# Head of a state-space and expert-routing kernel: unread matrix products in TensorE's gaps, and work moved between VectorE, GpSimd and ScalarE

## The reference, cut to what matters

```
mod = (silu(c) @ wmod)            -> sa, ca, ga, sb, cb, gb   (ga, gb clamped away from zero)
h   = layernorm(x) * (1 + ca) + sa
x   = x + ga * layernorm(h + mamba_f(h) + flip(mamba_b(flip(h)))) * ln_w + ln_b   (ga times all of the norm)
h   = layernorm(x) * (1 + cb) + sb
x   = x + gb * experts(h)          8 experts, each takes its top 64 tokens
```

## Time and profile before

| | us |
|---|---|
| three timed runs | 550.45, 551.61, 551.61 |
| median of the timed runs | 551.61 |
| profiled execution, its own time | 550.56 |
| profiled execution, its span | 548.8 |
| start of the first scan (line 1175) in the span | 46.25 |

### The profile page before, as it was taken

The page is one execution under the profiler, slowest core; times in us unless marked ns, Lnnn a source line. Parts: engine busy times, 40 slices in busy tenths (PEclk is TensorE's granted clock), DMA queues, the critical chain, the costliest instruction groups (busy, mean ns, idle before and its releaser), DMA issues.

```text
span 548.8 us, 9235 instructions
## 1 busy us (share of the span) xinstructions
PE 469.3 (86%) x3362; PEld 383.1 (70%) x3364; DVE 443.9 (81%) x681; ACT 437.9 (80%) x836; POOL 360.7 (66%) x190
## 2 busy tenths in 40 slices
PE   3577999998989899888999996979787867998897
PEld 3244866766769578777796585969776757677697
DVE  5888787858988687799888788799899999978741
ACT  1459897999996999999968999999998973266071
POOL 3104576876977987789689799999987868015000
PEclk9988999999999999999999998899999998999999
DMA  8021222221323222123322222232272321300011
GB/s 275 4 82 44 78 76 78 78 78 48 117 76 116 78 91 102 39 85 117 116 78 78 76 78 78 86 116 78 99 204 86 113 74 33 125 0 2 1 40 39
DMA packets 18255, 44.78 MB, mean 82 GB/s; under 512 B 1377, under 2 KB 7649, under 8 KB 17953
## 3 DMA queue, kind: packets, MB, share of 16 engines
q1 hardware_dynamic: 18208, 44.18, 24.0%
HBM read 42.61 MB, written 1.57 MB: 80 GB/s over the span
## 4 chain that ended last, share of the span: by engine, by line
ACT 42%; PE 30%; DVE 21%; issue 5%; POOL 1%; DMA 1%; DVEq 0%; ACTq 0%; POOLq 0%
ACT dBuT L733 20%; ACT dA L717 12%; PE pro L1389 9%; DVE area L1178 8%; PE yT L1389 7%; PE yT L1393 6%; PE dBu L1393 5%; PE dBu L1389 2%; DVE area L949 1%; ACT th L683 1%; ACT area L695 1%; ACT pre L692 1%; ACT area L707 1%; DVE area L1235 1%; ACT L717 1%
## 5 line engine op out<-in xcount | busy, mean ns | idle before, releaser
L604 POOL TENSOR_TENSOR hc<-area 128x1024 f32<-128x1024 f32 x127 | 300.1, 2373 | 101.8 <-DVE area L1175 62.9
L733 ACT ACTIVATE dBuT<-area,bT 128x256 f32<-128x256 f32 x492 | 208.7, 505 | 3.0 <-PE dBu L1393 3.0
L1393 PE MATMUL dBu<-ident,dBuT 128*128 128x128 f32 x992 | 140.0, 279 | 32.3 <-DVE area L1178 17.3
L717 ACT ACTIVATE dA<-area,Aneg 128x1024 f32<-128x1024 f32 x124 | 141.9, 1148 | 5.4 <-DVE area L1178 5.4
L1393 PEld LDWEIGHTS dBu<-ident,dBuT 128*128 128x128 f32 x992 | 112.1, 142 | 45.0 <-issue 16.2
L1393 PE MATMUL yT<-ident,hc 128*128 128x128 f32 x1024 | 136.6, 278 | 0.3 <-DVE hc L1316 0.3
L1393 PEld LDWEIGHTS yT<-ident,hc 128*128 128x128 f32 x1024 | 117.7, 143 | 18.2 <-issue 14.5
L1175 DVE TENSOR_TENSOR_SCAN area<-dA,dBu 128x512 f32<-128x512 f32 x62 | 74.7, 1205 | 13.1 <-PE dBu L1393 11.9
L1175 DVE TENSOR_TENSOR_SCAN area<-dA,area,dBu 128x512 f32<-128x512 f32 x62 | 79.2, 1278 | 5.0 <-PE dBu L1393 1.0
L1178 DVE TENSOR_TENSOR_SCAN area<-dA,area,dBu 128x512 f32<-128x512 f32 x62 | 79.2, 1277 | 3.9
L1178 DVE TENSOR_TENSOR_SCAN area<-dA,dBu 128x512 f32<-128x512 f32 x62 | 74.6, 1203 | 4.9 <-PE dBu L1393 4.5
(11 more groups left out here) (252 smaller groups left out, 569.9 us busy)
## 6 DMA issues: line engine op xcount, KB each, us to landing
area<-bc_rows SPq DMA_DIRECT2D x64, 512.0 KB, 3.7
dBuT<-w_in SPq DMA_DIRECT2D x1, 2048.0 KB, 9.4
wp<-wpack_in SPq DMA_DIRECT2D x1, 1030.0 KB, 7.1
x<-x_in SPq DMA_DIRECT2D x2, 512.0 KB, 6.4
hc<-bcast_in SPq DMA_DIRECT2D x1, 1024.0 KB, 10.3
Bb<-bc_rows SPq DMA_DIRECT2D x2, 512.0 KB, 3.9
out<-x SPq DMA_DIRECT2D x3, 256.0 KB, 2.4
bc_rows<-xdbl SPq DMA_DIRECT2D x4, 128.0 KB, 3.6
```

The lines of the kernel that those rows point to most:

```text
L604: g_.tensor_tensor(hc[:, e % 3, :], hs[:, e % 3, :], Cb[:, g % 3, :], ALU.mult).then_inc(hc_done, 1)
L717: nc.scalar.activation(dA[:, e % 3, :], delta[par][:, half, :], ACT.Exp, scale=Aneg[:, dr, half, s:s + 1]).then_inc(da_ready, 1)
L733: return nc.scalar.activation(dBuT[:, SCALED.index(g) % 2, n, :], duT[par][:, n, :], ACT.Copy, scale=bT[:, par, n, s:s + 1])
L1393: return nc.tensor.matmul(out, in_, ident[:, :] if idn is None else idn, start=start, stop=True, is_transpose=True, skip_group_check=True)
```

## The change

It touches the head only. Each part, as the diff has it:

- **Identity first.** GpSimd makes `ident` as its first and second instruction instead of its first and eighth.
- **Unread products.** A new helper `keep_going(dst, n)` on TensorE issues n products identity times identity of 128 columns, into columns 256 to 383 of the bank `dBu[0]`, which nothing reads. There are 14 once the identity is there, 4 behind the modulation products, 4 behind `turn_xn(0)`, 14 after the gate rows were kept and ahead of `turn_xn(1)`, and 6 behind `turn_xn(1)`.
- **Second batch's norm by GpSimd.** `x_norm(1)` leaves VectorE; GpSimd runs the same eight instructions behind its second power.
- **D blocks by GpSimd.** The four `dskip` instructions leave `other_weights` and run on GpSimd between its two powers, behind a wait for the packed weights and for `x_norm(0)`.
- **Gate rows by ScalarE.** The copy of the gate rows out of `dBu[0]` leaves VectorE; ScalarE does it after the last tap of both halves. The rows go to a place in `acc[:, 0]` instead of `acc[:, 1]`.
- **Second modulation later.** `modulate(1)` runs on ScalarE behind both tanh and ahead of the table load.
- **Tap weights in two halves.** `tap_weights` takes the direction as an argument: the forward four run ahead of `first_taps`, the backward four behind `other_weights`.

```
 GpSimd
             g_.memset(ident[:, :], 0.0).then_inc(s_c, 1)
+            g_.wait_ge(s_c, 1)
+            g_.affine_select(out=ident[:, :], in_=ident[:, :], compare_op=ALU.not_equal, fill=1.0, base=0,
+                             pattern=[[-1, P]], channel_multiplier=1).then_inc(s_c, 1)
             g_.memset(ones[:, :], 1.0).then_inc(s_c, 1)
...
-            g_.wait_ge(s_c, 7)
-            g_.affine_select(out=ident[:, :], in_=ident[:, :], compare_op=ALU.not_equal, fill=1.0, base=0,
-                             pattern=[[-1, P]], channel_multiplier=1).then_inc(s_c, 1)
...
+            def d_blocks():
+                g_.wait_ge(s_w, 16)
+                g_.wait_ge(xn_ready, 1)
+                for dr in range(2):
+                    for half in range(NH):
+                        at = WAT["dskip"] + dr * NH + half
+                        last = g_.tensor_scalar(dskip[:, dr, half, :], ident[:, :], wp[:, at:at + 1], None, ALU.mult)
+                last.then_inc(others_ready, 1)
...
                 g_.tensor_tensor(rstd[:, rs], rstd[:, rs], mhalf[:, rs], ALU.pow).then_inc(xrstd_ready, 1)
+                if b == 0:
+                    d_blocks()
+            g_.wait_ge(xrstd_ready, NB)
+            for n in range(NBLK):
+                r = NBLK + n
+                last = g_.tensor_scalar(acc[:, 1, n, :], x[:, 1, n, :], mv[:, r, 0:1], rstd[:, r:r + 1],
+                                        ALU.subtract, ALU.mult)
+            last.then_inc(xn_ready, 1)
 ScalarE
-            modulate(1)
+            act.wait_ge(gab_ready, 1)
+            nc.scalar.activation(gtemp[:, 0, :], dBu[0][:, 0:NB * D], ACT.Copy).then_inc(gab_kept, 1)
             act.wait_ge(parts_turned, 1)
...
                 nc.scalar.activation(th0[half], xc[0][:, half, :], ACT.Tanh).then_inc(th0_ready, 1)
+            modulate(1)
             nc.scalar.preload_act_table(ACT.Softplus)
 VectorE
             bias_parts()
             x_stats(1)
-            x_norm(1)
+            tap_weights(0)
             first_taps(0)
             first_taps(1)
             first_x(0)
             first_x(1)
             other_weights()
-            dve.wait_ge(xn_turned, 2)
-            keep_gate_rows()
-            tap_weights()
+            tap_weights(1)
             gate_rows()
 TensorE
+            def keep_going(dst, n):
+                for _ in range(n):
+                    mm(dst, ident[:, :], ident[:, :], True, True)
+            spare = dBu[0][:, 2 * P:3 * P]
+            pe.wait_ge(s_c, 2)
+            keep_going(spare, 14)
             pe.wait_ge(s_c, 10)
             pe.wait_ge(siluc_ready, 1)
...
+            keep_going(spare, 4)
...
             turn_xn(0)
+            keep_going(spare, 4)
...
             turn_parts()
+            pe.wait_ge(gab_kept, 1)
+            keep_going(spare, 14)
             turn_xn(1)
+            keep_going(spare, 6)
             pe.wait_ge(bias_ready, 1)
...
-            pe.wait_ge(weights_ready, 1)
-            pe.wait_ge(others_ready, 1)
+            pe.wait_ge(weights_ready, 2)
+            pe.wait_ge(others_ready, 2)
```

More of the change, by code:

```diff
@@ L389, in build_block @@
         convw = convrow.rearrange("p (d k c) -> p d k c", d=2, k=DC)
-        gtemp = acc[:, 1, 0:3 * NB, :].rearrange("p n d -> p (n d)").rearrange("p (i s) -> p i s", i=3)
+        gtemp = acc[:, 0, 0:3 * NB, :].rearrange("p n d -> p (n d)").rearrange("p (i s) -> p i s", i=3)
         convc = w("convc").rearrange("p (d h k) -> p d h k", d=2, h=NH)
@@ L780, in _ @@
                 if (k, j) == ("DU", 2):
-                    act.wait_ge(others_ready, 1)
+                    act.wait_ge(others_ready, 2)
                     exp_tile(0)
@@ L975, in bias_parts @@
                                         ALU.subtract).then_inc(parts_ready, 1)
-            def keep_gate_rows():
-                dve.wait_ge(gab_ready, 1)
-                nc.vector.tensor_copy(gtemp[:, 0, :], dBu[0][:, 0:NB * D]).then_inc(gab_kept, 1)
             def first_high_blocks():
@@ L988, in first_high_blocks, with tap_weights @@
                 last.then_inc(high0_ready, 1)
-            def tap_weights():
+            def tap_weights(dr):
                 dve.wait_ge(s_cw, 16)
[L993 to L996, removed]
+                for k in range(DC):
+                    last = nc.vector.scalar_tensor_tensor(wtap[:, dr, k, :], convw[:, dr, k, :], 0.5, inx[:, dr, :],
+                                                          ALU.mult, ALU.mult)
                 last.then_inc(weights_ready, 1)
@@ L1001, in other_weights @@
                 dve.wait_ge(aexp_ready, 1)
[L1002 to L1008, removed]
+                nc.vector.tensor_scalar(Aneg[:, :, :, :], Aneg[:, :, :, :], -1.0, None, ALU.mult).then_inc(others_ready, 1)
             def clamp_gate(out, g, sign, size):
```

## The result

| | us |
|---|---|
| changed kernel, 20 runs | median 549.29, 546.69 to 555.74 |
| kernel before, 20 runs beside it | median 550.74, 550.16 to 556.56 |
| ratio of the two | 0.9947, 95% interval 0.9924 to 0.9970 |
| profiled execution of the changed kernel | 548.6, span 546.7 |

By the ratio the change is worth 2.9 us, with an interval of 1.7 to 4.2 us (ratio times 551); the medians are 1.5 us apart, the lowest runs 3.5. These differ because neither set of runs is symmetric: 15 of the 20 of the kernel before lie between 550.16 and 551.61, and five at 553.7 to 556.6; those of the changed kernel are spread over 6 us. The slow run of 555.74 is left out of the ratio. The forecast was 4.7 us and 546.3. Four runs are there (546.69, 546.75, 546.88, 546.95); the median is 3.0 us above, and 0.5 above the end of the range.

A forecast was written before the change was run, and what follows sets the result against it. The head's chain of waits, with TensorE at its low clock level, was taken as the bound; 0.94 + 1.87 + 1.92 = 4.73 us off a mean of 551.06 gave 546.3, range 544.5 to 548.8.

The forecast's parts named there:

- Fourteen products: TensorE's start: 14 unread products take 6.3 us at the low level, end by 7.8, cost nothing and raise the clock.
- Transposes, projection, B items: TensorE in the head: at the high clock level these gain 0.94, 1.87 and 1.92 us.
- Shifted whole: Everything from 34.47 on, loop included, moves earlier by the head's whole gain of 4.73 us.
- The table load: ScalarE ahead of B 0: load of 1.28 us ends at 28.65, hidden by 0.2; rival of lateness 0.9 us, chance 0.02.
- Norm of batch 1 on GpSimd: Eight instructions at 0.448 us behind the second power: 3.6 us, to 20.6; bounds 2.1 and 7.2.
- one of the signs that I had named for a wrong forecast: Ahead of the B items: the forecast is wrong if TensorE isn't idle just ahead of them.
- Is VectorE free by then?: VectorE ahead of the taps: done with forward tap weights at 16.6, 0.4 us before the taps start at 17.08.
- Without these moves it would be late by 1.3 us.: VectorE's gate steps: without moving D blocks, gate rows' copy and backward tap weights, VectorE would be 1.3 us late.
- I take it as unchanged; between 2 us gained and 1 lost.: Clock fall in TensorE's 2.85 us idle gap before the first scan: may come or not, counted as no change.
- the loop takes the gain back: Rival, loop: stream starts 4.7 us earlier but meets a worse clock fall or later wait; about 550, chance 0.07.
- The clock as high "from before 7.9": TensorE's clock counted as high from before 7.9, ahead of the modulation products, after the 14 early products.
- the clock falls again: Rival, ahead of B items or while ScalarE holds TensorE: late 548.2, chance 0.07; low at 19.3, 550.5, chance 0.04.

The follow-up runs named there:

- the second profile of the kernel before: The kernel before timed and profiled once more, no edit: median 550.38 us over 9 runs, ratio 0.9976 to itself.
- the second profile of the changed kernel: The changed kernel timed and profiled once more, no edit: median 549.10 us over 12 runs, ratio 0.9945 to the kernel before; profiled execution 549.13.
- the norm's form: Changed kernel with GpSimd's norm of batch 1 as one multiply-add, x times rstd plus a per-token shift: median 549.19 us, ratio 0.9959.
- denser early products: Changed kernel with more unread products at the start, between and behind the modulation products, and behind batch 0's transposes: median 548.27 us, ratio 0.9912.
- all three: Changed kernel with multiply-add norm on GpSimd, denser early products and two gaps filled: median 547.07 us over 6 runs, ratio 0.9896.
- two gaps filled: Changed kernel with 12 more unread products ahead of the first scan and 9 ahead of the first Z item: median 547.66 us, ratio 0.9930.

## Why the prediction was right and wrong

Where it was right, by its own steps:

- *Fourteen products.* Foretold 6.3 us at the low price to 7.8; 5.94 to 7.52. The clock was up behind them.
- *Transposes, projection, B items.* 0.94, 1.87 and 1.92 us were foretold. Measured: 1.98 - 1.10 = 0.88; the projection's half 0 is done when the last tap starts, 16.08 - 14.02 = 2.06 against 18.65 - 14.80 = 3.85, so 1.79; 5.55 - 3.64 = 1.91. Without the products the transposes are back at 1.97, half 0 at 3.49 and the B items at 5.03 us; the last two are 0.4 and 0.5 below the rows that I counted from, and the same in the second profile of the kernel before (3.47 and 5.02).
- *Shifted whole.* -4.46 stays -4.4 over 380 us of loop.
- *The table load* held ScalarE no longer than its row: 27.50 to 28.78, and ScalarE then waited 0.37 us for B 0. The drain that the Trainium skill adds to a load ("ScalarE: Activation LUTs", What ACT_TABLE_LOAD costs) isn't seen here either: B 0 was copied at 29.16.

Where it was off:

- *Norm of batch 1 on GpSimd.* "I take 3.6": 6.22 us, near the upper bound of 7.2. I called line 579 the same form because its operands are; its operations (multiply, add) are not those of the norm (subtract, multiply). B came at 26.34 and not at 26.09, but hardly through this: with the norm done at 21.6 it came at 26.30, so the norm cost 0.04 us and the late taps the rest. What it did use up is the slack: TensorE was idle for 0.09 us ahead of the B items and not for 1.2, which was one of the signs that I had named for a wrong forecast. VectorE's taps had no part in it: the other form kept its price beside the same taps, in agreement with what the prediction took from the Trainium skill ("GPSIMD Engine Reference", Key points).
- *Is VectorE free by then?* At 16.90 instead of 16.6: two of its small casts beside GpSimd's D blocks took 0.28 and 0.31 instead of 0.17 us, and its norm ended 0.1 later. It still waited 0.41 us for ScalarE, so this isn't why the taps start at 17.31 instead of 17.08; that comes from the transposes (0.1 late and 0.06 longer) and half 0 of the projection. D blocks 2.37 instead of 1.8, hidden.
- *"Without these moves it would be late by 1.3 us."* With the D blocks and tap weights back on VectorE (the gate rows' copy stayed on ScalarE) its first softplus product was 0.8 us late and the first scan 0.14.
- *"I take it as unchanged; between 2 us gained and 1 lost."* This is the step that failed, the term for the falls of the clock behind the head: put at nothing, it measures 2.4 us in the first profile (0.5 at 416.6, 1.9 at 491.6) and 2.2 in the second (1.65 at 53.7, 0.3 at 419, 0.25 at 494), where another 0.7 is lost in the head. I gave it one place, the gap ahead of the first scan, where it costs 0.5 us at the scan (42.20 against 41.73 with it filled) that the loop has back by 50 us. The profiles show six others: the modulation products (0.7 us in the second profile of the changed kernel, 1.4 in that of the norm's form), the delta products (1.9, denser early products), the first D products (1.6, second profile), the unit change at 121 (0.85, all three), the loop near 417 to 423 (0.3 to 0.5, in four profiles), the tail (1.9 in the first profile, 2.2 with two gaps filled). That the runs without a profile lose their time in the same way is argued from their clock and from the fastest ones, which take 546.6 to 546.9. The rival "the loop takes the gain back" (0.07, about 550) named "a worse fall of the clock or a later wait"; the first half of it is what came.
- *The clock as high "from before 7.9"* holds only until it falls again: my count had the transposes safe once it was up, and the rival "the clock falls again" looked only at the B items and what is ahead of them. Six profiles have the early products as the change has them. In four of them the clock fell again between 8.8 and 10.1 us, while or just after the two-column modulation products ran; in the first and that of the two filled gaps it did not.
- *The base of the sum.* The rows come from one profile of the kernel before, whose head was 1.1 us behind that of the second. How much of the 4.46 us a typical run gains isn't known; the two profiles of before give 4.5 and 3.4.

What stays open: why most runs of the kernel before meet falls that cost little, and what sets the place. The falls that cost time stand mostly behind an idle stretch of TensorE (2.3 us idle ahead of the fall at 53.7, 2.2 ahead of that at 121, 0.77 ahead of those at 492 to 498), but the same stretch is followed by a fall in one profile and not in another: that of 0.77 us in 7 of the 14. In the two kernels that were profiled twice, those of the loop that both profiles have are moved together, by 1.6 us in the kernel before and by 2.4 in the changed one. The program's order is the same in both, so it doesn't set the place alone; what else does isn't shown.

## What to carry to other kernels

Unread products raised TensorE's clock here, but a head with some gaps left kept it in some executions and not in others: fill the stretches between narrow products too, and each gap ahead of the path's next wide products, and then look at the spread of the runs, not only at one profile. That holds for the profile of before as well: count from two of them, since a gain read off one carries its chance (1.1 us here). A higher clock on one engine pays only as far as the queues beside it are cleared first: products alone and moves alone were both worth nothing here; together they brought the median down by 1.5 us (2.9 by the ratio), and with the remaining gaps filled by 3.7 and 3.9. A price from a row holds for the operations in it, not for its shape.

## What the runs showed of the hardware that I had not expected

- GpSimd's tensor_scalar on 128 x 128 fp32 with two per-partition scalars takes 0.79 us for subtract and multiply, 0.45 for multiply and add; with one scalar (multiply alone) 0.61.
- The column of the granted clock reads 1.00 from the start of the trace to the first fall, also where the pace is that of the low level: in the changed kernel's profile 28 records of 128 columns take 5.94 us, 0.212 each, at the start, and 28 take 3.39 us, 0.121 each, later.
- A row in which TensorE looks nearly full is no promise of the high level: ahead of the fall at 491.6 TensorE was busy for 3.23 us of 488 to 492, with products of 8 and 64 columns. The same stretch went without a fall in 7 of the 14 profiles.
